# Deeper gather ring, sort turns behind quarters of a tile, and one-hots built from one tensor and two columns of scalars

## The chip, the cores and the metric

The kernel runs on one core of a Trainium2 chip. The core has a matrix engine (TensorE, PE in the profile), three elementwise engines (VectorE or DVE, ScalarE or ACT, GpSimd or POOL), and a queue engine that issues transfers (SyncE or SP). The metric is the device time of one execution in microseconds; shorter is better.

## The reference, cut to what matters

A graph step and a small network. The graph step is the part that the change touches:

```python
h = _layernorm(x) @ weight.T                 # x: 8192 nodes x 512
msgs = edge_weight[:, None] * h[dst]         # 131072 edges
x = x + segment_sum(msgs, src, num_segments=8192)
x = x + ffn(_layernorm(x))                   # seven layers of 160 on a few columns, one-hot results
```

Each edge takes row `dst` of `h`, scales it, and adds it to row `src` of `x`. The edges arrive sorted by `dst`, and have to be added by `src`.

## The kernel before, in words

**Stage one, the product.** `h` is computed in 64 tiles of 128 rows. `multiply(n)` makes four f32 matmuls of 512 columns for tile n, out of `xT` (8 tiles in flight) and `wT`; ScalarE scales the result (`h_rows_out`) and SyncE stores it to `h_dram`. Beside it ScalarE makes the statistics of x, on which `s_sd` tells.

**The sort.** The edges are cut into 4 parts of 128 partitions x 256 (NC) edges. VectorE sorts each part by `src` with a bitonic network: 113 exchange stages. A stage is a "keys" slot (compare into `swap`, L950; copy of the weights, L956; minimum, L958) and a "weights" slot (maximum, L962; predicated copy of the weights, L964). Between stages along the free axis and stages along partitions all keys and weights are transposed on TensorE, 15 times per part (`turn_edges`, L1328 and L1334). During stage one ScalarE copies the turned keys and weights back to SBUF (`turn_out`, L708 and L710); later VectorE copies the turned keys itself (L987). `flip` changes the sign of some keys ahead of a round. The list SORT_SLOTS holds all this in order; every engine walks the same list. Then come "index" (L991, from which POOL may begin to gather the part), "source", and the sums "maxima", "counts", "rows" that make a staircase: tables of which tile of nodes (`tile_of`) and which chunk of 128 edges a step joins, and when a chunk or a tile ends.

`plan()` lays the sort of part 0 and the head of part 1's sort beside stage one. It adds up fixed prices for VectorE and TensorE and gives BEHIND_TILE: behind which tile each turn stands in TensorE's program. HEAD is the number of slots of part 1 that are done before stage two.

**Stage two, the aggregation.** POOL issues 1024 indirect gathers (L630), one per chunk of 128 sorted edges: 128 rows of h, 2 KB each, into one slot of a ring. In parts 0 and 1 the ring has WIDE = T - KEPT + RING = 42 slots: the room of x tiles 32 to 63 (x of those nodes waits in DRAM) and of `wT`, `xT`. In parts 2 and 3 it has RING = 10 slots. Each part has 319 steps (NS). Step i joins one chunk to one tile of nodes: VectorE builds a 128 x 128 matrix with the edge weights at the right rows (`build`, L1064), TensorE multiplies it with the gathered chunk into the PSUM bank of the tile (`add_step`, L1452), up to SR = 8 builds ahead. ScalarE seeds and reads out the banks. A gather into a used slot waits till the steps of the chunk in it are done (`slot_free`). The sort slots of the next part are laid between the steps (`slots_with_steps`), to be through LAST_STEPS = 40 steps before the part begins. Two waits of POOL matter here:

```python
if c == 0:
    pool.wait_ge(s_sd, LOADS)
    near_rows_stored()
if c + 1 == T - KEPT:
    pool.wait_ge(s_mm, T)        # slots under wT and xT: free when stage one is over
```

**Stage three** is the network: it packs marked nodes, runs seven layers, adds the one-hots, and stores.

Of the kernel before, what the change touches and what calls it, by code (L numbers as in the profile page):

```python
# [7 lines left out]
I32 = mybir.dt.int32  # L8
# [7 lines left out]
def gnn_ffn(nc, x, src, dst, edge_weight, gnn_w, ffn_w, ffn_b, x_blocks, out):  # L16
# [8 lines left out]
    P = 128  # L25
# [13 lines left out]
    RING = 10  # L39
    KEPT = 32  # L40
# [4 lines left out]
    FILLED = 44  # L45
# [7 lines left out]
    LAST_STEPS = 40  # L53
# [11 lines left out]
    FAR_BEHIND = 2  # L65
# [9 lines left out]
    def sort_slots():  # L75

        yield "pack", 0, 0
        for k in range(1, QB + 1):
# [5 lines left out]
            yield "flip", k, 0  # L84
# [12 lines left out]
        yield "source", 0, 0  # L97
        for what in ("maxima", "counts", "rows"):
# [7 lines left out]
    ON_TENSOR = ("turn", "maxima summed", "counts summed", "rows summed")  # L106
    assert sum(what == "turn" for what, _, _ in SORT_SLOTS) == TURNS
    assert sum(what == "weights" for what, _, _ in SORT_SLOTS) % 2 == 1

    def plan():  # L110
# [7 lines left out]
        end = start + T * tile + turn * (TURNS + 3)  # L118
        head, is_open = 0, False
        for g in range(2):  # L120
            for at, (what, _, _) in enumerate(SORT_SLOTS):
# [3 lines left out]
                if what in ON_TENSOR:  # L125
                    while n < T - 1 and tensor + tile / 2 < vector:
                        tensor, n = tensor + tile, n + 1
                    behind.append((n, g, what))
                    vector = tensor = max(vector, tensor)
                    vector, tensor = vector + turn, tensor + turn  # L130
# [3 lines left out]
                vector += vector_times.get(what, 0.0)  # L134
                inverts.append(0)
                while b < LOADS and (vector > start + (b * LT + 1) * tile or what in ON_TENSOR and b <= n // LT):
# [15 lines left out]
    BEHIND_TILE, INVERTS, HEAD = plan()  # L152
    HEAD_TURNS = sum(what == "turn" for what, _, _ in SORT_SLOTS[:HEAD])
# [19 lines left out]
    with ctx:  # L173
# [12 lines left out]
        AT_DATA = AT_IOTA + N // 2  # L186
        AT_SORT = AT_DATA + PARTS * 3 * NC
        AT_TAB = AT_SORT + 4 * NC
# [16 lines left out]
        carve = carver(0, AT_EARLY)  # L205
        wT = carve(KD * D).rearrange("p (k f) -> p k f", k=KD)
        all_xT = carve(XS * D)
        xT = all_xT.rearrange("p (s k n) -> p s k n", s=XS, k=KD)
        w_load = all_xT[:, (XS - KD) * D:XS * D].rearrange("p (k f) -> p k f", k=KD)
        carve = carver(AT_EARLY, AT_IOTA)  # L210
# [28 lines left out]
        parts = [(carve(NC, I32), carve(NC), carve(NC)) for _ in range(PARTS)]  # L239
# [1358 lines left out]
```

## Time and profile before

| | us |
|---|---|
| median of 3 runs | 1632.9 (1631.47 to 1633.22) |
| the profiled execution, its own time | 1631.87 |
| its span, first to last instruction | 1630.0 |
| stage one: first to last matmul of L1318 | 15.3 to 244.6 |
| gathers: first and last issue | 192.6 and 1522.3 |
| stage three | about 1529 to 1630 |

The span is 1.9 us below the execution's own time, and that is 1.0 us below the median. The profile's busy share is an average over three stages with different limits: what counts is which wait ends last in each.

### The profile page before, as it was taken

To read this page: it belongs to the slowest core of one execution; us is meant where nothing else is said; L and a number is where in the kernel's file an instruction comes from. 1 tells how busy PE (TensorE), PEld (TensorE's weight loads), DVE (VectorE), ACT (ScalarE), POOL (GpSimd) and SP (SyncE) were. 2 spreads that over 40 slices of the span, in tenths; PEclk is the share of its full clock that TensorE was granted. 3 is DMA by queue.
4 is the path that set the end of the run, shared out by engine and by line. 5 is a ranking of instruction groups with operands and counts; after the bars stand their busy time and mean duration, and the time that the engine had idled before them with its cause. 6 is when DMAs were issued, how large, how long until landed. Compare 5 with 4: busy or idle time off the path is not lost.

```text
span 1630.0 us, 27821 instructions
## 1 busy us (share of the span) xinstructions
PE 1522.7 (93%) x3697; PEld 619.9 (38%) x3698; DVE 1116.9 (69%) x4106; ACT 556.9 (34%) x1223; POOL 1070.4 (66%) x1099
## 2 busy tenths in 40 slices
PE   7999998999989899999998999998999999999995
PEld 3444443444333234343333433333433333333442
DVE  8776648788877878888778777787433333336885
ACT  7887212222222222222222222222234444444332
POOL 2000257777777777777777777777777777777970
PEclk9999999999999999999999999999999999999998
DMA  9886687777999877789988777888877777777563
GB/s 334 300 280 227 213 271 216 205 202 220 307 309 302 285 202 207 199 251 324 309 297 257 207 215 202 246 258 253 252 206 212 209 210 210 208 210 203 181 208 110
DMA packets 162798, 387.79 MB, mean 238 GB/s; under 512 B 32642, under 2 KB 51362, under 8 KB 162466
## 3 DMA queue, kind: packets, MB, share of 16 engines
q0 software_dynamic: 81920, 268.50, 55.4%
q1 hardware_dynamic: 57666, 75.51, 13.8%
q10 hardware_dynamic: 23040, 41.95, 7.7%
q8 instruction: 51, 0.84, 0.2%
q14 instruction: 121, 0.99, 0.2%
HBM read 335.54 MB, written 55.57 MB: 240 GB/s over the span
## 4 chain that ended last, share of the span: by engine, by line
PE 80%; DVE 10%; issue 5%; DMA 2%; DVEq 2%; ACT 0%; POOL 0%; SPq 0%; POOLq 0%; ACTq 0%
PE psum L1452 60%; PE psum L1318 14%; PE psum L1484 3%; DVE rows L1064 3%; DMA rows<-h_rows,rows 2%; DVE rows L964 2%; DVEq L1064 1%; DVE rows L950 1%; DVE rows L956 1%; DVE rows L1144 1%; PE psum L1328 1%; PE psum L1334 1%; DVE rows L962 1%; DVE rows L958 1%; DVE rows L1209 0%
## 5 line engine op out<-in xcount | busy, mean ns | idle before, releaser
L630 POOL DMA_INDIRECT rows<-h_rows,rows x1024 | 1007.7, 984 | 506.2 <-issue 399.3
L1452 PE MATMUL psum<-rows 128*128 x2552 | 1186.2, 608 | 77.5 <-DVE rows L1064 35.3
L1452 PEld LDWEIGHTS psum<-rows 128*128 128x128 f32 x2552 | 443.8, 189 | 775.3 <-issue 767.4
L1064 DVE SCALAR_TENSOR_TENSOR rows<-rows 128x128 f32 (+1 forms) x1276 | 444.9, 351 | 384.4 <-PE psum L1452 271.8
L792 ACT ACTIVATE rows<-psum 128x512 f32<-128x512 f32 x128 | 76.4, 597 | 479.3 <-PE psum L1452 479.3
L1318 PE MATMUL psum<-rows 128*128 128x512 f32 x512 | 223.2, 593 | 0.8 <-ACT rows L689 0.8
L964 DVE COPY_PREDICATED rows<-rows 128x256 f32<-128x256 int32 x407 | 179.7, 442 | 0.0
L774 ACT ACTIVATE psum<-rows 128x512 f32<-128x512 f32 x256 | 153.7, 601 | 8.0
L950 DVE TENSOR_TENSOR rows<-rows 128x128 int32<-128x128 f32 x452 | 129.5, 287 | 19.8 <-ACT rows L708 18.2
L1318 PEld LDWEIGHTS psum<-rows 128*128 128x128 f32 x512 | 96.0, 190 | 114.7 <-issue 114.7
L962 DVE TENSOR_TENSOR rows<-rows 128x128 f32<-128x128 f32 x452 | 128.8, 285 | 0.2
L958 DVE TENSOR_TENSOR rows<-rows 128x128 f32<-128x128 f32 x452 | 128.3, 284 | 0.1
L956 DVE COPY rows<-rows 128x256 f32<-128x256 f32 x407 | 120.5, 296 | 0.6 <-DVE rows L950 0.6
L790 ACT ACTIVATE rows<-psum 128x512 f32<-128x512 f32 x64 | 38.2, 597 | 241.3 <-PE psum L1452 241.3
L828 ACT ACTIVATE rows<-psum 128x512 f32<-128x512 f32 x64 | 38.2, 597 | 181.0 <-PE psum L1452 181.0
L698 ACT ACTIVATE rows<-psum,x_rstd 128x512 f32<-128x512 f32 x64 | 43.9, 686 | 84.2 <-PE psum L1318 83.4
L1484 PE MATMUL psum<-rows 96*96 96x432 f32 x160 | 64.1, 548 | 0.1
L639 POOL TENSOR_SCALAR rows<-rows 128x512 f32<-128x512 f32 x64 | 54.1, 856 | 0.0
L853 ACT ACTIVATE rows<-psum,bias 96x432 f32<-96x432 f32 x48 | 29.6, 616 | 47.7 <-PE psum L1484 44.4
L652 ACT ACTIVATE rows<-rows,x_neg 128x512 bf16<-128x512 f32 x64 | 45.6, 716 | 0.5
L839 ACT ACTIVATE psum<-rows,neg_mean 128x512 f32<-128x512 f32 x64 | 44.2, 691 | 2.1
L652 ACT ACTIVATE rows<-rows 128x512 bf16<-128x512 f32 x68 | 41.8, 620 | 4.5 <-DMA rows<-in_L_gnn_weight 4.5
(152 smaller groups left out, 493.1 us busy)
## 6 DMA issues: line engine op xcount, KB each, us to landing
rows<-in_x_blocks SPq DMA_DIRECT2D x32, 512.0 KB, 4.4
rows<-in_x SPq DMA_DIRECT2D x16, 1024.0 KB, 7.2
h_rows<-rows SPq DMA_DIRECT2D x64, 256.0 KB, 2.9
rows<-h_rows,rows POOLq DMA_INDIRECT x1024, 3.9
summed_rows<-rows ACTq DMA_DIRECT2D x64, 256.0 KB, 5.4
rows<-summed_rows ACTq DMA_DIRECT2D x64, 256.0 KB, 4.4
out<-rows SPq DMA_DIRECT2D x4, 2816.0 KB, 10.7
rows<-in_x ACTq DMA_DIRECT2D x32, 256.0 KB, 5.3
```

Source lines behind the costliest of these rows:

```text
L630: pool.indirect_dma_start(into[:, (c + 1) % n_slots, :], None, h_dram, bass.IndirectOffsetOnAxis(ap=dst_i[g][:, i:i + 1], axis=0),).then_i ...
L652: act.activation(junk[:, sums[0] % 2, :], a, func, bias=bias, accum_out=into).then_inc(s_sum, 1)
L774: act.activation(bank((u + 1) % AGG), given, ACT.Copy).then_inc(s_seed, 1)
L950: dve.tensor_tensor(swap, low, high, ALU.is_gt).then_inc(s_sort[g], 1)
L956: dve.tensor_copy(weights[1 - now], weights_now).then_inc(s_sort[g], 1)
L958: dve.tensor_tensor(to_low, low, high, ALU.min).then_inc(s_sort[g], 1)
L962: dve.tensor_tensor(to_high, low, high, ALU.max).then_inc(s_sort[g], 1)
L964: dve.copy_predicated(both(weights[1 - now], j), swap.unsqueeze(2).to_broadcast(both(weights_now, j).shape), both(weights_now, j)[:, :, :: ...
L1064: dve.scalar_tensor_tensor(spread[:, slot % SR, :], iota_n[:, bass.ds((tile - (g * T + 1)) * P, P)], src_f[g][:, bass.ds(chunk - (g * NC + ...
L1318: last = pe.matmul(bank(n % 4), xT[:, n % XS, k, :], wT[:, k, :], start=(k == 0), stop=(k == KD - 1))
L1452: pe.matmul(banks[:, bass.ds(pe.snap(tile_wanted) % AGG, 1), :].rearrange("p t f -> p (t f)"), spread[:, slot % SR, :], landed_in[:, bass. ...
L1484: return pe.matmul(halves(l)[e], fwT[:, d, l - 1, half_rows[e]], act_f[:, (l - 1) % 2, d, :], start=(d == 0), stop=(d == 1))
```

## The change

- **Ring.** KEPT 32 to 20 and RING 10 to 14: WIDE goes from 42 to 58 slots. 44 tiles of x instead of 32 wait in DRAM; ScalarE's queue loads and stores them. `xT` moves into the last 8 slots of the ring and `wT` out of it, so POOL waits for the end of stage one at chunk 49 instead of chunk 31. The wait on all statistics at chunk 0 becomes one for each x tile whose room a chunk takes. FILLED 44 to 36 (14 fills of rows of `h_dram` instead of 10, two at a time).
- **Turns.** `plan()` has new prices and places turns behind a quarter of a tile (BEHIND_BLOCK) instead of a whole one. VectorE takes the turned weights and the lower half of the turned keys straight from PSUM and copies only the upper half; ScalarE's two copies are gone. The flips ahead of the rounds along partitions become one multiplication by a column of signs in the last stage ahead of the turn (`flip_rows`).
- **Records in the order of steps.** New slot "steps": matmuls with one-hots (`step_hots`) put, for each part, node row and weight of every step in columns (`step_rows`, `step_weights`). "source" is gone.
- **Build.** It reads no table and no register: one tensor and two columns of scalars in the place of two tensors and one column.
- **Far row.** The greatest `dst` of part 0 is found by POOL (`tensor_reduce` over all axes) instead of VectorE and TensorE. POOL's first iota has 1023 columns instead of 8192.
- LAST_STEPS 40 to 64.

```diff
-    RING = 10
-    KEPT = 32
+    RING = 14
+    KEPT = 20
...
-    FILLED = 44
+    FILLED = 36
...
-    LAST_STEPS = 40
+    LAST_STEPS = 64
...
+    def flips_behind(k, j):
+
+        return k >= 7 and k < QB and j == 0
...
-        vector_times = {"pack": 6.0, "flip": 0.3, "keys": 0.65, "weights": 0.65, "turned": 1.9, "maxima": 2.5,
-                        "counts": 2.0, "rows": 2.0, "index": 0.4, "source": 0.8}
-        turn, tile, start = 0.9, 3.43, 15.5
+        vector_times = {"pack": 6.7, "flip": 0.38, "keys": 0.6, "weights": 0.556, "turned": 0.0, "maxima": 3.6,
+                        "counts": 2.0, "rows": 3.2, "steps": 1.0, "index": 0.4}
+        turn, of_block, back, start = 0.75, 0.8575, 0.8, 15.5
...
+            pool.wait_ge(s_edge[0][1], 16)
+            pool.tensor_copy(far_f, dst_i[0]).then_inc(s_far_f, 1)
+            pool.wait_ge(s_far_f, 1)
+            pool.tensor_reduce(far_one[:, :], far_f, mybir.AxisListType.XYZWC, ALU.max).then_inc(s_far, 1)
...
                 if c == 0:
-                    pool.wait_ge(s_sd, LOADS)
                     near_rows_stored()
-                if c + 1 == T - KEPT:
+                if KEPT + c + 1 < T:
+                    pool.wait_ge(s_sd, (KEPT + c + 1) // LT + 1)
+                if c + 1 == WIDE - XS:
                     pool.wait_ge(s_mm, T)
...
-                        if turns <= BY_SCALAR[g]:
-                            dve.wait_ge(s_key_in[g], turns)
-                        else:
-                            weights_now = turned_weights
-                            dve.wait_ge(s_turn_k[g], turns)
-                            dve.tensor_copy(keys_now, turned_keys).then_inc(s_key_in[g], 1)
-                            dve.wait_ge(s_key_in[g], turns)
+                        weights_now, is_turned = turned_weights, True
+                        dve.wait_ge(s_turn_k[g], turns)
+                        first = 6 if j else k - 1
+                        dve.tensor_copy(pairs(keys_now, first)[1], pairs(turned_keys, first)[1]).then_inc(s_key_in[g], 1)
+                        dve.wait_ge(s_key_in[g], turns)
...
-                if i % MORE == 0:
-                    dve.reg_load(walk, tile_of[row_of(g), i:i + MORE])
-                of_tile, of_chunk = ranges(g, i)
-                dve.reg_alu(minus_tile, walk[i % MORE], -1, ALU.mult)
-                dve.reg_alu(of_step, minus_tile, g * T + 1 + g * NC + 1 + i, ALU.add)
-                tile = dve.snap(walk[i % MORE], **of_tile)
-                chunk = dve.snap(of_step, **of_chunk)
                 slot = g * NS + i
                 if slot >= SR:
                     dve.wait_ge(s_done, slot + 1 - SR)
-                dve.scalar_tensor_tensor(spread[:, slot % SR, :], iota_n[:, bass.ds((tile - (g * T + 1)) * P, P)],
-                                         src_f[g][:, bass.ds(chunk - (g * NC + 1), 1)],
-                                         weight[g][:, bass.ds(chunk - (g * NC + 1), 1)].to_broadcast([P, P]),
-                                         ALU.is_equal, ALU.mult).then_inc(s_op, 1)
+                dve.tensor_scalar(spread[:, slot % SR, :], row_q[:, :], step_rows[g][:, i:i + 1],
+                                  step_weights[g][:, i:i + 1], ALU.is_equal, ALU.mult).then_inc(s_op, 1)
...
+            def sum_steps(g):
+
+                pe.wait_ge(s_fin[g], 3)
+                rows_sum, share_sum = bank(ROW_BANK)[:, 0:NSP], bank(SHARE_BANK)[:, 0:NSP]
+                pe.matmul(rows_sum, turned_src[:, 0:P], step_hots[:, 0, :], start=True, stop=False)
+                pe.matmul(rows_sum, turned_src[:, P:NC], step_hots[:, 1, :], start=False, stop=False)
+                pe.matmul(rows_sum, ones[0:T, :], over, start=False, stop=True)
+                pe.matmul(share_sum, turned_wgt[:, 0:P], step_hots[:, 0, :], start=True, stop=False)
+                pe.matmul(share_sum, turned_wgt[:, P:NC], step_hots[:, 1, :], start=False, stop=True).then_inc(s_stair[g], 1)
```

## Rows read from the trace of the kernel before

**Rows 1.** The page: busy time by engine, and the chain that ended last by engine.
```profile
PE 1522.7 (93%) x3697; PEld 619.9 (38%) x3698; DVE 1116.9 (69%) x4106; ACT 556.9 (34%) x1223; POOL 1070.4 (66%) x1099
...
PE 80%; DVE 10%; issue 5%; DMA 2%; DVEq 2%; ACT 0%; POOL 0%; SPq 0%; POOLq 0%; ACTq 0%
```

**Rows 2.** Timeline of POOL: start, length, what, idle time before it (us).
```profile
192.62 1.17 POOL L630 DMA_INDIRECT rows<-h_rows,rows  x1 [183.26 <-issue]
...
232.89 0.95 POOL L630 DMA_INDIRECT rows<-h_rows,rows  x1 [0.30 <-issue]
245.35 0.94 POOL L630 DMA_INDIRECT rows<-h_rows,rows  x1 [11.52 <-PE psum L1318]
...
1522.32 0.95 POOL L630 DMA_INDIRECT rows<-h_rows,rows  x1 [0.30 <-issue]
```

**Rows 3.** Gathers by stretch: its length, busy time (count), granted clock, DMA share.
```profile
245.20:560.00 314.80, 241.00 (x242) 0.99 0.82 256
560.00:870.00 310.00, 236.78 (x241) 1.00 0.83 258
...
1180.00:1440.00 260.00, 197.25 (x207) 1.00 0.73 209
```

**Rows 4.** Weight copies L956, one for each exchange stage, by stretch.
```profile
245.20:560.00 314.80, 37.68 (x120) 0.99 0.82 256
560.00:870.00 310.00, 34.40 (x112) 1.00 0.83 258
```

**Rows 5.** Steps built (L1064) in part 0 and in part 1.
```profile
246.00:561.00 315.00, 110.39 (x318) 0.99 0.83 257
561.00:873.00 312.00, 110.72 (x319) 1.00 0.83 258
```

**Rows 6.** Waits of VectorE up to 192 us: in all, times, longest.
```profile
DVE rows L942 <- ACT rows L708: 18.3, 7, 3.9
DVE rows L950 <- ACT rows L708: 18.2, 7, 4.2
```

**Rows 7.** Timeline of VectorE: two stages in a row, and part 0's "index".
```profile
98.56 0.29 DVE L950 TENSOR_TENSOR rows<-rows 128x128 int32<-128x128 f32 x1
...
99.71 0.29 DVE L950 TENSOR_TENSOR rows<-rows 128x128 int32<-128x128 f32 x1
...
190.48 0.29 DVE L991 TENSOR_SCALAR rows<-rows 128x256 int32<-128x256 int32 x1
```

**Rows 8.** Timeline of TensorE in stage one: 40 matmuls, a turn, the end.
```profile
15.32 34.57 PE L1318 MATMUL psum<-rows 128*128 128x512 f32 x80 [0.78 <-ACT rows L689]
49.73 0.38 PE L1328 MATMUL psum<-ident,rows 128*128 128x128 f32 x2
...
50.16 0.27 PE L1376 MATMUL psum<-ident,far_col 128*1 128x128 f32 x1
...
235.42 9.18 PE L1318 MATMUL psum<-rows 128*128 128x512 f32 x21
```

**Rows 9.** Timeline of the start: POOL's long iota, and VectorE's first pack operation.
```profile
1.19 6.95 POOL L576 IOTA rows<- 128x8192 int16 x1
...
6.93 1.51 DVE L912 TENSOR_SCALAR rows<-rows 128x256 int32<-128x256 int32 x1 [5.00 <-DMA rows<-in_src]
```

**Rows 10.** Timeline: a gather beside a build, a weight copy, and a flip.
```profile
1270.12 0.35 DVE L1064 SCALAR_TENSOR_TENSOR rows<-rows 128x128 f32 x1 [1.06 <-PE psum L1452]
1270.26 1.04 POOL L630 DMA_INDIRECT rows<-h_rows,rows  x1 [0.30 <-issue]
...
990.27 1.08 POOL L630 DMA_INDIRECT rows<-h_rows,rows  x1 [0.30 <-issue]
...
990.91 0.28 DVE L956 COPY rows<-rows 128x256 f32<-128x256 f32 x1
...
1015.29 0.95 POOL L630 DMA_INDIRECT rows<-h_rows,rows  x1 [0.30 <-PE psum L1452]
1015.33 0.22 DVE L942 TENSOR_SCALAR rows<-rows 128x128 f32<-128x128 f32 x1
```

More of the change, by code:

```diff
@@ L96, in sort_slots @@
         yield "index", 0, 0
-        yield "source", 0, 0
-        for what in ("maxima", "counts", "rows"):
+        for what in ("maxima", "counts", "rows", "steps"):
             yield what + " summed", 0, 0
@@ L134, in plan @@
                 vector += vector_times.get(what, 0.0)
+                if what == "weights" and flips_behind(k, j):
+                    vector += 0.25
                 inverts.append(0)
-                while b < LOADS and (vector > start + (b * LT + 1) * tile or what in ON_TENSOR and b <= n // LT):
+                while b < LOADS and (vector > start + (b * LT + 1.7) * tile or what in ON_TENSOR and b <= n // (KD * LT)):
                     inverts[-1], b = inverts[-1] + 1, b + 1
@@ L150, in gnn_ffn @@
     assert FIRST_HOTS + QT // 2 < FIRST_PACK
-    BEHIND_TILE, INVERTS, HEAD = plan()
-    HEAD_TURNS = sum(what == "turn" for what, _, _ in SORT_SLOTS[:HEAD])
+    BEHIND_BLOCK, INVERTS, HEAD = plan()
     def slots_with_steps():
@@ L246, in gnn_ffn @@
         below = other_weights[:, 0:NC // P * T]
-        over = rest[0:T, 0:NSP]
+        over = rest[0:T, 2 * NC - NSP:2 * NC]
+        turned_src, turned_wgt = carve(NC), carve(NC)
+        step_hots = region[:, AT_SORT:AT_SORT + 2 * NSP].rearrange("p (b i) -> p b i", b=2)
+        assert 2 * NSP <= 4 * NC - NSP and NC == 2 * P
         carve = carver(AT_TAB, REGION)
@@ L444, in progress @@
             steps = turns = buffer = 0
-            for what, _, _ in SORT_SLOTS:
+            for what, k, j in SORT_SLOTS:
                 if what == "turn":
@@ L449, in progress @@
                     turns += 1
-                steps += SORT_STEPS.get(what, 0)
+                steps += steps_of(what, k, j)
                 buffer ^= what == "weights"
@@ L492, in _ @@
                         load_pair(n // 2 + XS // 2)
-                    late = next(to_fill, None) if n >= 2 * (LOADS - FIRST_LOADS) else None
-                    if late is not None:
+                    for late in islice(to_fill, 2 if n >= 2 * (LOADS - FIRST_LOADS) else 0):
                         sp.dma_start(h_dram[late * P:(late + 2) * P, :], x[late * P:(late + 2) * P, :]).then_inc(s_fill, 16)
@@ L992, in sort_edges @@
                                           ).then_inc(s_index, 1)
-                    elif what == "source":
-                        src_i = keys[1 - now].bitcast(I32)
-                        step(dve.tensor_scalar(src_i, keys[now].bitcast(I32), KEY, N - 1,
-                                               ALU.logical_shift_right, ALU.bitwise_and))
-                        dve.tensor_copy(src_f[g], src_i).then_inc(s_fin[g], 1)
                     elif what == "maxima":
@@ L1318, in multiply @@
                     last = pe.matmul(bank(n % 4), xT[:, n % XS, k, :], wT[:, k, :], start=(k == 0), stop=(k == KD - 1))
-                last.then_inc(s_mm, 1)
+                    if k == KD - 1:
+                        last.then_inc(s_mm, 1)
+                    for block, g, what in BEHIND_BLOCK:
+                        if block == KD * n + k:
+                            of_sort(g, what)
             def turn_edges(g, turn):
@@ L1382, in of_sort @@
                     sum_rows(g)
+                elif what == "steps summed":
+                    sum_steps(g)
             turn_w()
@@ L1386, in _ @@
                 multiply(n)
-                for tile, g, what in BEHIND_TILE:
-                    if tile == n:
-                        of_sort(g, what)
             def turn_layer(l):
```

182 lines of the change are left out of this document (102 added, 80 removed).

## The prediction

> **What bounds the kernel now.** The page comes first, and it misleads: TensorE is busy 93% of the span and holds 80% of the chain that ended last, POOL is busy 66% and holds none of it [rows 1]. The timeline of POOL shows the bound. The first gather is issued at 192.6 us, one wait of 11.5 us ends when stage one does, and from 245.35 us to 1522.32 us there follow 992 more, each with the same 0.30 us of idle time ahead of it and nothing longer [rows 2]. That is 1277.0 / 992 = 1.287 us a gather. POOL waits for no slot and for no sort: in stage two it is never stopped, and nothing that doesn't touch its pace or its start can move 1522.3 us, behind which the last steps and stage three take a fixed 107.7 us (to 1630.0). TensorE runs in its shadow: its small waits for chunks, spread over the steps, are what the chain adds up as TensorE.
>
> Gathers by stretch show what the pace is made of [rows 3]: without sort beside it one takes 197.25 / 207 = 0.953 us, with sort 0.996 and 0.983. The excess over 0.953 is 10.4 + 7.2 = 17.6 us in two stretches with 232 stages [rows 4]: a stage of five VectorE operations costs POOL 0.076 us, or 15 ns an operation.
>
> **The ring and its wait.** The sum starts where POOL is stopped. Before, 31 gathers are out when stage one ends; after, POOL may issue 49. Their start is early enough: "index" stands at 190.5 us [rows 7], and it moves forward (below, to about 165), while 49 gathers take 49 x 1.3 = 64 us. So at the end of stage one POOL stands 18 chunks further: 18 x 1.287 = -23.2 us. The start of the gathers by itself is worth nothing: POOL then waits for the end of stage one some 25 us instead of 11.5. The other conditions (36 tiles stored, 14 fills, statistics) are met near tile 38, at about 155 us, and bind less than "index". The 24 more stores and 36 more loads of 256 KB run on ScalarE's queue beside a DMA share of 0.8; the gathers have the same length at 0.82 as elsewhere, so I cost them at nothing; what hides them is a ring 13 deep or more. Without that cover each late chunk would cost its lateness.
>
> **The end of stage one.** It is at 235.42 + 9.18 = 244.6 us [rows 8]. A matmul takes (49.73 - 15.32) / 40 = 0.86 us, a turn 50.16 - 49.73 = 0.43 us. The new plan puts four more turns (part 1's) ahead of the end: 1.7 us. sum_steps is five matmuls of 320 columns, 5 x 0.54 = 2.7 us, and two more transposes 0.1 us. Unhindered, stage one ends at 249.1 us: the lower bound.
>
> But every turn stands at a fixed place in TensorE's program and waits for VectorE's sort. Before, VectorE was always early and waited: 18.3 + 18.2 = 36.5 us over 14 turns, 2.6 us each [rows 6]. After, the turns are set by VectorE's expected pace, and TensorE waits where it is late; behind TensorE's wait the rest of stage one is queued, and behind that POOL. VectorE's path to "index": 190.5 less the waits (36.5), less the start that POOL's iota held up (1.2, below), less the far operations (seven short ones, about 1.6), plus 15 turns at 0.8 us (0.4 for the transposes of the keys, 0.3 for half a copy, 0.1 for semaphores), plus 3 for full-width flips and PSUM operands: 166 us. Walking plan() with its own prices gives 159.1 us there, and the last turn of part 1's head behind block 226 at 228.8 us. VectorE is thus some 5 us late (7 less 2 of slack where the plan lets it wait), and the end is 228.8 + 5 + 0.4 + 29 x 0.86 = 259 us; if the plan is right, 254. Between 249.1 and 260 I take 257, near the VectorE end, because it sets the pace in most turns: +12.4 us.
>
> **The stages moved.** HEAD goes from 28 slots to 130: 45 stages of part 1 instead of 12 are done in stage one. 33 x 0.076 = -2.5 us of POOL's excess. VectorE has little work late in stage one today, which is the cover for this.
>
> **The build.** Its time on VectorE is not on POOL's path; what it does to gathers is. A build today starts at 1270.12 and runs over the start of a gather at 1270.26, which takes 1.04 instead of 0.945 us: it ends 0.83 us behind the build. In the stretch without sort builds are nearly alone: (0.953 - 0.945) x 207 = 1.7 us for 258 steps, 7 ns a build. The new form reads one tensor. The nearest rows are the copy L956 and the flip L942, also of one tensor, which run at two elements a cycle by their lengths (256 in 0.28, 128 in 0.22 us). Behind the copy at 990.91 the gather of 990.27 takes 1.08 us, and ends again a fixed time (0.15) behind it; beside the flip at 1015.33 the gather stays at 0.95 [rows 10]. So the new build may also hold a gather at a later point, and is shorter (0.28 to 0.35). Bounds for the difference: -7 ns (it never holds one) and +15 ns (as an operation of the sort), -9 to +19 us over 1276. I take +4 ns, the flip being nearer in form than the copy: +5 us.
> The Trainium skill (SBUF - State Buffer, section "SBUF: two separate sides") says that a VectorE operation in a two-port mode and a GpSimd operation exclude each other for the whole instruction. The rows show less: most overlapped gathers keep 0.945 us. By the rule each build met by a gather would stop it, and the sum would end well on the slower side.
>
> **On VectorE itself** the build loses 0.0 to 0.07 us and its register work; "maxima", "rows" and "steps" gain some 3 us a part and "source" loses 0.6. LAST_STEPS moves part 1's end of sort from step 279 to 255. None of it is on POOL's path while sorts are done in time.
>
> **Sum.** -23.2 + 12.4 - 2.5 + 5 = -8.3 us. The profiled execution: 1631.87 - 8.3 = 1623.6; the median stands 1.0 higher: 1624.6 us.
>
> **Rivals.**
> *The steps can't follow (no gain or slower).* In part 2 the ring shrinks to 14 slots, and gather 517 needs the slot of chunk 507, whose last step is about number 632. POOL is there at 257.7 + 468 x 1.287 = 860 us. Steps begin at 259.3, so they must take 0.950 us or less. Today they take 627 / 637 = 0.984 us [rows 5], although the ring is full enough: TensorE waits for builds queued behind sort slots. It has 0.86 us plus 24 turns and the sums, 0.895. VectorE loses 33 stages (38 us at 1.15 us [rows 7]), some of each build, and the register work. I expect 0.935. At an unchanged pace the stop is 259.3 + 632 x 0.984 - 860 = 21 us, and the time 1646. It decides from 0.950 us on. Chance 0.19, spread over 1625 to 1646.
> *POOL's reduction holds VectorE (slower).* The iota on POOL runs to 8.14 us, and VectorE's operation of 6.93, which takes 0.29 elsewhere [rows 7], ends 0.30 us behind it [rows 9]. The new tensor_reduce starts at about 9 us, when the sort does. Nothing in the rows prices it: at least the 0.4 us of an operation of 256 columns; if it walks partition by partition at iota's 6.95 / 8192 us an element, 32768 elements take 28 us. Turns wait for VectorE, so each microsecond goes to the end of stage one and to POOL: 1624.6 + 28 = 1652. It decides from 8 us on. Against it: the new plan prices the pack at 6.7 us. Chance 0.14.
> The Trainium skill (GPSIMD Engine Reference, "Cross-partition - where GPSIMD wins") measures 247,699 ns for a partition reduction of [128, 2048]; an estimate by columns is 31 us for 256. No run here shows it yet.
> *Builds hold gathers often (slower).* At one in five and 0.15 us, as the long gathers of [rows 10] suggest, 1276 builds cost 38 us instead of 5: 1658. The gain is gone from 10 ns a build on. Chance 0.10.
> *More gain.* TensorE hardly waits (end at 250) and builds cost nothing: -23.2 + 5.4 - 2.5 - 4 = -24: 1609. Chance 0.09.
> *The parts cancel* within 3 us, by a few waits of each kind: 0.08.
>
> **How the numbers follow.** The forecast, with 1618 to 1631 as its own range, has 0.40. The range of 1608 to 1656 leaves out less than 2 in 10: the ends of the last rivals but one. A difference of 0.2%, 3.3 us, is about what a measurement of this kernel can tell from none. Faster: 0.37 of the forecast, 0.09, and 0.02 of the first rival: 0.48. Same: 0.03, 0.08 and 0.05: 0.16. Slower: 0.36.
>
> **What would show it.** POOL's timeline: first gather near 165, one long wait ahead of gather 49, ended by TensorE at about 257; any later wait ahead of gather 517 or so is the first rival. Gathers of 0.95 us in the stretch without sort, where 0.97 and more would be the third. The reduction's length at 9 us and VectorE's copies beside it. TensorE's waits for VectorE in stage one: some 8 us. The last gather at about 1514. The forecast is wrong if POOL has a second stop, or if its 0.30 us between gathers changes.

## The result, and the profile after

The changed kernel takes 1689.4 us (median of 4 runs, 1674.8 to 1696.3) against 1632.2: a ratio of 1.0339, interval 1.0271 to 1.0408. Ratios here compare only the runs of a kernel that lie within 1.5% of its fastest, while medians and ranges are of all its runs. It is 3.4% slower where 0.5% faster was forecast, and outside the range. The profiled execution has a span of 1686.8 us; 1621.7 was forecast (1630.0 - 8.3), 65.1 us less. The experiments ran on four chips, each time beside the kernel before, whose median lies between 1634 and 1650 us there: from one chip to another the ratios compare better than the times.

The page of the changed kernel, as [rows 1]:
```profile
PE 1540.3 (91%) x3744; PEld 639.6 (38%) x3745; DVE 1109.3 (66%) x4158; ACT 548.6 (33%) x1193; POOL 1118.6 (66%) x1102
...
PE 71%; DVE 21%; issue 5%; DMA 2%; POOL 0%; ACT 0%; POOLq 0%; SPq 0%; DVEq 0%
```
POOL is 48 us busier and VectorE has 21% of the chain instead of 10%. POOL's timeline, as [rows 2], says where:
```profile
166.29 1.19 POOL L662 DMA_INDIRECT rows<-h_rows,rows  x1 [157.79 <-DMA h_rows<-rows]
...
256.96 0.96 POOL L662 DMA_INDIRECT rows<-h_rows,rows  x1 [21.42 <-PE psum L1337]
...
1560.34 0.95 POOL L662 DMA_INDIRECT rows<-h_rows,rows  x1 [0.30 <-issue]
```
The first gather (165 forecast), one stop ahead of the fiftieth, its end (257.7 forecast): all as foreseen, and no second stop. But the 974 gathers behind it have a pitch of (1560.34 - 256.96) / 974 = 1.338 us, not 1.287, so that the last comes 46 us behind the forecast 1514. The idle time between them is still 0.30 us; the gathers themselves are longer. By stretch, as [rows 3]:
```profile
258.00:560.00 302.00, 235.56 (x218) 1.00 0.85 270
560.00:870.00 310.00, 241.90 (x223) 0.99 0.82 253
870.00:1140.00 270.00, 209.33 (x199) 0.99 0.78 233
1180.00:1440.00 260.00, 196.63 (x209) 1.00 0.75 218
```
And the weight copies, one for each stage of the sort (L982 now), as [rows 4]:
```profile
258.00:560.00 302.00, 30.74 (x102) 1.00 0.85 270
560.00:870.00 310.00, 29.62 (x98) 0.99 0.82 253
```
Without sort beside it a gather takes 0.941 us, no more than before (cut-off gathers left out, the mean is 0.948 us, and 0.956 in the kernel before): the new build holds hardly any, as 10 gathers of this stretch are longer than 0.96 us, where it was 28 before. With sort it takes 1.081 and 1.085. That excess is 30.4 + 32.1 = 62.5 us over 200 stages, 0.31 us a stage, where [rows 3, 4] had 0.076.

The rest of the 65 us is behind the last gather: 126.4 us to the end instead of 107.7. Timelines of POOL and of VectorE there:
```profile
1561.32 39.73 POOL L671 TENSOR_SCALAR rows<-rows 128x512 f32<-128x512 f32 x48
```
```profile
1566.68 19.64 DVE L1163 TENSOR_SCALAR rows<-rows 128x216 bf16<-128x216 int16 x1 [8.78 <-PE psum L1480]
```
One small VectorE operation (its fifteen fellows take 6.3 us together) needs 19.64 us, while POOL runs its scalings without a break. In the kernel before POOL runs them without a break as well, from the same 0.99 us behind the last gather, and the sixteen operations together take 6.40 us. Timelines of POOL and of VectorE before:
```profile
1523.31 21.86 POOL L639 TENSOR_SCALAR rows<-rows 128x512 f32<-128x512 f32 x24
```
```profile
1529.03 6.40 DVE L1144 TENSOR_SCALAR rows<-rows 128x216 bf16<-128x216 int16 x16 [3.88 <-PE psum L1452]
```

### The profile page after: what moved, and what is told of

It is laid out like the page before. It is cut to its first block, busy times and chain, and to the rows that moved or that the text cites. A ratio compares the mean times of both kernels' runs of the same rounds, so it can differ in the third digit from the quotient of the medians.

```text
span 1686.8 us, 24194 instructions
## 1 busy us (share of the span) xinstructions
PE 1540.3 (91%) x3744; PEld 639.6 (38%) x3745; DVE 1109.3 (66%) x4158; ACT 548.6 (33%) x1193; POOL 1118.6 (66%) x1102
## 4 chain that ended last, share of the span: by engine, by line
PE 71%; DVE 21%; issue 5%; DMA 2%; POOL 0%; ACT 0%; POOLq 0%; SPq 0%; DVEq 0%
PE psum L1480 53%; PE psum L1337 11%; DVE rows L1085 4%; DVE rows L994 3%; PE psum L1512 3%; DVE rows L982 3%; DVE rows L978 2%; DVE rows L984 2%; DVE rows L988 2%; DVE rows L1163 2%; DMA rows<-h_rows,rows 1%; PE psum L1349 1%; DVE rows L1006 1%; PE psum L1353 0%; POOL rows L662 0%
## 5 line engine op out<-in xcount | busy, mean ns | idle before, releaser
L662 POOL DMA_INDIRECT rows<-h_rows,rows x1024 | 1062.2, 1037 | 490.6 <-issue 225.2
L1480 PEld LDWEIGHTS psum<-rows 128*128 128x128 f32 x2552 | 455.1, 190 | 782.0 <-issue 772.5
L1085 DVE TENSOR_SCALAR rows<-row_q,rows 128x128 f32<-128x128 f32 x1276 | 440.8, 356 | 308.3 <-PE psum L1480 287.8
L994 DVE COPY_PREDICATED rows<-rows 128x256 f32<-128x256 int32 x392 | 171.2, 437 | 0.0
L1337 PEld LDWEIGHTS psum<-rows 128*128 128x128 f32 x512 | 95.5, 190 | 112.6 <-issue 112.4
L1006 DVE COPY rows<-psum 128x128 f32<-128x128 f32 x60 | 17.5, 291 | 167.1 <-PE psum L1349 166.9
L982 DVE COPY rows<-rows 128x256 f32<-128x256 f32 x392 | 116.0, 296 | 0.0
L978 DVE TENSOR_TENSOR rows<-rows 128x128 int32<-128x128 f32 x392 | 110.2, 281 | 0.8
L988 DVE TENSOR_TENSOR rows<-rows 128x128 f32<-128x128 f32 x392 | 110.0, 281 | 0.0
L984 DVE TENSOR_TENSOR rows<-rows 128x128 f32<-128x128 f32 x392 | 109.9, 280 | 0.1
L1512 PE MATMUL psum<-rows 96*96 96x432 f32 x160 | 67.9, 575 | 0.1
```

What stands on the lines that cost most here:

```text
L662: pool.indirect_dma_start(into[:, (c + 1) % n_slots, :], None, h_dram, bass.IndirectOffsetOnAxis(ap=dst_i[g][:, i:i + 1], axis=0),).then_i ...
L978: dve.tensor_tensor(swap, low, high, ALU.is_gt).then_inc(s_sort[g], 1)
L982: dve.tensor_copy(weights[1 - now], weights_now).then_inc(s_sort[g], 1)
L984: dve.tensor_tensor(to_low, low, high, ALU.min).then_inc(s_sort[g], 1)
L988: dve.tensor_tensor(to_high, low, high, ALU.max).then_inc(s_sort[g], 1)
L994: dve.copy_predicated(both(weights[1 - now], j), swap.unsqueeze(2).to_broadcast(both(weights_now, j).shape), both(weights_now, j)[:, :, :: ...
```

## A lock between two engines

What makes the gathers long is seen where six long ones follow each other. POOL's timeline of the changed kernel:
```profile
654.14 1.36 POOL L662 DMA_INDIRECT rows<-h_rows,rows  x1 [0.30 <-issue]
655.80 1.35 POOL L662 DMA_INDIRECT rows<-h_rows,rows  x1 [0.30 <-PE psum L1480]
657.45 1.35 POOL L662 DMA_INDIRECT rows<-h_rows,rows  x1 [0.30 <-issue]
```
and VectorE's beside it, one stage of the sort with its two builds:
```profile
654.39 0.28 DVE L984 TENSOR_TENSOR rows<-rows 128x128 f32<-128x128 f32 x1
654.59 0.34 DVE L1085 TENSOR_SCALAR rows<-row_q,rows 128x128 f32<-128x128 f32 x1
654.85 0.28 DVE L988 TENSOR_TENSOR rows<-rows 128x128 f32<-128x128 f32 x1
655.05 0.44 DVE L994 COPY_PREDICATED rows<-rows 128x256 f32<-128x256 int32 x1
655.39 0.34 DVE L1085 TENSOR_SCALAR rows<-row_q,rows 128x128 f32<-128x128 f32 x1
655.64 0.28 DVE L978 TENSOR_TENSOR rows<-rows 128x128 int32<-128x128 f32 x1
655.85 0.28 DVE L982 COPY rows<-rows 128x256 f32<-128x256 f32 x1
656.05 0.28 DVE L984 TENSOR_TENSOR rows<-rows 128x128 f32<-128x128 f32 x1
```
L978 is the comparison, L982 the weight copy, L984 the minimum, L988 the maximum, L994 the predicated copy. Each starts some 80 ns before the one ahead of it has ended: there is no break. The minimum ends at 654.67 and the gather of 654.14 at 655.50, 0.82 us behind it (the rows are rounded); the gather of 655.80 ends at 657.15, 0.82 us behind the next minimum (656.33). So a gather that is held ends 0.82 us behind a minimum, the next starts 0.30 us later, and by then (1.12 us behind the minimum) the next stage has begun (0.97 us behind it). It is held again, and the gathers take the stage's period, 1.66 us, for their own 1.25. I call that the lock. Told by this arithmetic alone (held again if the next stage begins within 1.12 us) it is theory 4 of the expectations, formed after e8; e10 will refute the arithmetic, not the lock.

It can be counted. For all gathers issued from 262 to 1150 us: held is one longer than 0.953 us that ends 0.78 to 0.835 us behind a minimum. "Next stage" is the median time from a minimum's end to the next comparison's start. The mean is of all gathers behind the end of stage one, with sort beside them or not; the time is the median of all runs.

| run | next stage, us | held | of them followed by a held one | mean gather, ns | median time, us |
|---|---|---|---|---|---|
| before | 1.175 | 67 | 3 | 983 | 1632 |
| after | 0.975 | 140 | 98 | 1033 | 1689 |
| e1 | 0.971 | 150 | 108 | 1041 | 1697 |
| e2 | 0.986 | 131 | 93 | 1047 | 1708 |
| e3 | 0.984 | 130 | 93 | 1048 | 1703 |
| e4 (before, fixed) | 0.984 | 134 | 93 | 1050 | 1717 |
| e5 | 1.166 | 143 | 65 | 1026 | 1664 |
| e6 | 1.092 | 155 | 102 | 1034 | 1702 |
| e7 (before, fixed) | 1.104 | 141 | 84 | 1035 | 1703 |
| e8 | 0.972 | 154 | 111 | 1038 | 1675 |
| e9 | 1.239 | 31 | 0 | 974 | 1638 |
| e10 | 1.114 | 11 | 0 | 974 | 1634 |
| e11 | 1.239 | 28 | 0 | 975 | 1613 |
| e12 | 0.976 | 128 | 86 | 1029 | 1712 |
| e13 | 1.114 | 10 | 0 | 974 | 1615 |
| e14 (before, fixed) | 1.130 | 24 | 0 | 977 | 1647 |
| e15 | 1.239 | 36 | 0 | 974 | 1639 |
| e16 | 1.091 | 68 | 0 | 976 | 1640 |

The kernel before beside these took 1650 (e1 to e4), 1636 (e5 to e8), 1634 (e9 to e12) and 1642 us (e13 to e16; one of its 27 runs there took 8840.7 us). In the changed kernel held gathers make up 56 of the 83 us by which the gathers of the table exceed 0.945 us each; in the kernel before 18 of 31.

## The experiments

The theories at first: (1) the register work of the old builds left gaps on VectorE, in which gathers got through; (2) the form of the build; (3) something else in the change.

**e1.** Register work put back, unused:
```
...
+if i % MORE == 0:
+    dve.reg_load(walk, tile_of[row_of(g), i:i + MORE])
+dve.reg_alu(minus_tile, walk[i % MORE], -1, ALU.mult)
+dve.reg_alu(of_step, minus_tile, g * T + 1 + g * NC + 1 + i, ALU.add)
```


> The changed kernel with one thing put back: VectorE's queue again loads the tile numbers (one register load in every group) and works out two register values ahead of every build, as before; nothing reads them, and the build itself stays the new one-tensor form at fixed columns. Theory 1, gaps: before, this register work left about 0.10 us of VectorE's time empty between the last sort operation of a slot and the build, and in such a gap a gather that stands ready gets its start; the changed kernel has no gap there, the sort operations run back to back and hold gathers until their chain ends. Then the gap comes back here, the gathers' mean falls from 1.037 us towards 0.985, the last gather comes near 1515 to 1525 instead of 1560, and the time is near 1640 to 1650 (about 45 us less than the changed kernel). Theory 2, the form of the build: the old build read two tensors and was itself the place where gathers started or were let go in step; then nothing comes back here, mean 1.03 to 1.04 and 1680 to 1695. Theory 3, the rest of the change (the ring, the turned copies, the sort's new order) causes it: also 1680 to 1695.


Ratio 1.0267 (1.0204 to 1.0330), mean 1041 ns: nothing came back.

**e2.** The old form, fixed columns:
```
-dve.tensor_scalar(spread[:, slot % SR, :], row_q[:, :], step_rows[g][:, i:i + 1],
-                  step_weights[g][:, i:i + 1], ALU.is_equal, ALU.mult).then_inc(s_op, 1)
+dve.scalar_tensor_tensor(spread[:, slot % SR, :], row_q[:, :], step_rows[g][:, i:i + 1],
+                         step_weights[g][:, i:i + 1].to_broadcast([P, P]), ALU.is_equal, ALU.mult).then_inc(s_op, 1)
```


> The changed kernel with the build back as an operation on two tensors (the row numbers, and the weight's column broadcast along the row), at fixed columns and without register work. Theory 1 (gaps from register work): no gap comes back, gathers' mean stays 1.03 to 1.04 and the time 1680 to 1695, or some 5 us more if the build itself holds gathers. Theory 2 (the form of the build): the gathers' mean falls to about 0.985 and the time to 1640 to 1650. Theory 3 (the rest of the change): 1680 to 1695.


1708 us beside 1650, mean 1047 ns. Even its fastest run, 1680.2 us, lies above the slowest of the kernel before, 1654.0: theory 2 falls.

**e3.** Both.


> The changed kernel with both put back: register work ahead of every build and the build on two tensors. All else (ring of 14, order of steps, turns, far rows) is the change's. Theories 1 and 2 both give a gathers' mean near 0.985, the last gather near 1515 to 1525 and 1635 to 1650. Theory 3 (the rest of the change makes gathers longer): mean 1.03 or more, 1680 to 1700.


Ratio 1.0290 (1.0217 to 1.0363): neither. But the build still starts 202 ns behind the minimum's start, where it was 390 in the kernel before: the register work, whose results nobody read, ran hidden and made no gap. e1 and e3 hadn't tried theory 1.

**e4.** The kernel before, builds at fixed addresses, no register work; it leaves out the choice of the right columns:
```
...
-iota_n[:, bass.ds((tile - (g * T + 1)) * P, P)], src_f[g][:, bass.ds(chunk - (g * NC + 1), 1)], ...
+iota_n[:, 0:P], src_f[g][:, i % NC:i % NC + 1], weight[g][:, i % NC:i % NC + 1].to_broadcast([P, P])
```


> The kernel before with its build at fixed addresses and without the register work ahead of it; the form on two tensors stays. It leaves out the choice of the right columns, so its output isn't the reference's; the amount of work in the engines is the same but for the register work. Theory 1 (the register work made the gaps in which gathers start): the gathers' mean rises from 0.984 to 1.02 to 1.04 us, and the kernel gets slower by 30 to 50 us, 1660 to 1685. Theories 2 and 3: no slower, 1625 to 1635.


Ratio 1.0369 (1.0289 to 1.0450), which is 61 us of 1650 (67 between the medians), with every other part of the old kernel in place. The distance from minimum to build fell from 390 to 202 ns, and 93 of 134 held gathers are followed by a held one. So the loss needs no other part of the change: it comes when the addresses out of registers go, with their register work, which e1 and e3 found to do nothing by itself. Not all of it is the gathers': their pitch is 1.354 us instead of 1.287, and from the last gather to the end it is 132.7 us instead of 107.7, with one VectorE operation of 16.77 us in it.

**e5.** The changed kernel, builds addressed through registers (always to the same columns), with the register work that this needs:
```
...
+none = dve.snap(minus_tile, min_val=0, max_val=1)
+at = dve.snap(of_step, min_val=i, max_val=min(i + 1, NSP - 1))
-row_q[:, :], step_rows[g][:, i:i + 1], step_weights[g][:, i:i + 1]
+row_q[:, bass.ds(none, P)], step_rows[g][:, bass.ds(at, 1)], step_weights[g][:, bass.ds(at, 1)]
```


> In e1 and e3 the register work put back was hidden: the build still started 202 ns after the minimum of a sort stage, without a gap, so they didn't try theory 1. In the kernel before the gap of 105 ns stood ahead of builds whose columns come out of registers, and e4, without them, lost the gap and 67 us. Here the changed kernel gets register work and builds whose three operands are addressed through registers (they always come to the same columns as the fixed ones); the form stays the new one on one tensor. Theory 1 (a gap in VectorE's chain lets POOL's waiting gather start): the start of the build lies about 390 ns behind that of the minimum (L984 here), the gathers' mean falls from 1.037 to about 0.985, and the time comes near 1640 to 1655. Theory 3 (something else of the change makes gathers longer): the gap is there, the mean stays at 1.03 or more, the time 1685 to 1705.


The gap is back (391 ns from minimum to build); the time is 1663.7, ratio 1.0161 (1.0134 to 1.0189): about half of the loss. But hardly by the gathers. The last one comes at 1554.4 us, 6 us before that of the changed kernel, and their pitch is 1.331 us instead of 1.338; 19 us are won behind it, where it is 107.4 us to the end instead of 126.4 and no operation is long.

**e6.** The changed kernel with a wait behind the minimum:
```
 dve.tensor_tensor(to_low, low, high, ALU.min).then_inc(s_sort[g], 1)
 done += 3
+dve.wait_ge(s_sort[g], done)
```


> The changed kernel with one wait more in each sort stage: behind the minimum VectorE waits for its own completion before it goes on to the build. It should leave a gap of about 35 ns, as between other operations that wait for the one just ahead, and cost VectorE some 115 ns a stage, with 500 stages 58 us of a queue that idles for longer than that behind the gathers. Theory 1: gathers find the gap, mean about 0.985 to 1.0, 1640 to 1660 (slower by 0 to 10 than that if 35 ns is short for some). Theory 3: mean 1.03 or more, 1690 to 1710.


Ratio 1.0345 (1.0288 to 1.0402). The wait leaves 37 ns, and changes nothing for the gathers: their pitch is 1.338 us as without it. (It also stands in stage one, where it delayed the first gather to 180.7 us and the fiftieth to 272.8.)

**e7.** e4 with that wait.


> The kernel of e4 (the one before with builds at fixed addresses; it leaves out the choice of the right columns) and the same wait behind the minimum of each sort stage. Theory 1: the gap comes back, gathers' mean from 1.049 to about 0.985 to 1.0, and the time from 1717 to 1645 to 1670. If it was something else in the register work than the gap, it stays at 1700 to 1725.


Ratio 1.0393 (1.0352 to 1.0435): no. "Gaps" as such don't explain it; the column "followed by a held one" came out of these runs.

**e8.** The tail:
```
 pool.wait_ge(s_mark, h + 1)
+if h:
+    pool.wait_ge(s_hotf, h + 1)
```


> The changed kernel with POOL held, ahead of its 8 scalings of each later quarter of the tail, until VectorE has made the one-hots of that quarter. In the changed kernel POOL ran 32 of these back to back behind the last gather (24 us), and one VectorE operation beside them took 19.6 us instead of some 0.3. If that is what made the last stage 126.5 us instead of 107.7, the stage behind the last gather falls by 10 to 19 us and the time to 1670 to 1682 (gathers' mean unchanged at 1.03 to 1.04). If the long operation is an effect without cost, the time stays at 1685 to 1697.


1674.7 us (1674.0 to 1675.6), 14.7 less, and four runs within 1.6 us; by the ratios, 1.0236 instead of 1.0339, it is 17 us. 106.5 us from the last gather to the end, 19.9 less. Timelines of POOL and of VectorE in e8:
```profile
1567.02 12.42 POOL L673 TENSOR_SCALAR rows<-rows 128x512 f32<-128x512 f32 x16
1579.87 15.45 POOL L673 TENSOR_SCALAR rows<-rows 128x512 f32<-128x512 f32 x16 [0.43 <-DVE rows L1165]
```
```profile
1572.14 7.55 DVE L1165 TENSOR_SCALAR rows<-rows 128x216 bf16<-128x216 int16 x16 [8.49 <-PE psum L1482]
```
The sixteen operations take 7.55 us instead of 25.98.

**e9.** Waits behind minimum and predicated copy, beside the gathers alone (`spaced` is set behind stage one):
```
 dve.tensor_tensor(to_low, low, high, ALU.min).then_inc(s_sort[g], 1)
 done += 3
+if spaced:
+    dve.wait_ge(s_sort[g], done)
...
 dve.copy_predicated(...).then_inc(s_sort[g], 1)
 done += 2
+if spaced:
+    dve.wait_ge(s_sort[g], done)
```


> Theory 4, a lock, formed from the runs so far: a gather that becomes ready while the sort's two-input operations run back to back ends about 0.82 us behind the end of the minimum; the next gather starts 0.30 us later, 1.12 us behind that end. If the next stage's first operation has begun by then, that gather is held too. Time from the end of a minimum to the start of the next stage, median: 1.175 us in the kernel before (3 of 67 held gathers followed by a held one), 1.166 in e5 (65 of 143), 1.092 in e6 (102 of 155), 0.975 in the changed kernel (98 of 140), 0.984 in e4 (93 of 134). Here the changed kernel waits for its own completion behind the minimum and behind the predicated copy of a stage, in the second sort beside the gathers alone: the time is to be about 1.22 us. Theory 4: hardly any held gather is followed by a held one (under 15 in 100), the gathers' mean falls to 0.98 to 1.00, and the time to 1640 to 1655. Rival, gaps in general (the more empty time on VectorE, the more gathers get through): a second gap takes the mean from e6's 1.034 to 1.02 at best, time 1675 to 1690. Rival, neither: 1690 or more.


As theory 4 had it: no held gather is followed by a held one, the mean is 974 ns, the last gather comes at 1504.4 us. Median 1638.0 us, ratio 0.9926 (0.9883 to 0.9969). More waiting on VectorE made the kernel some 50 us faster.

**e10.** The second of the two waits alone.


> The same wait behind the predicated copy alone (second sort, beside the gathers): the time from the end of a minimum to the next stage is to be about 1.10 us, short of what a gather needs. Theory 4: still locked, more than half of the held gathers followed by a held one, mean 1.03 to 1.04, 1685 to 1700. Gaps in general: as for e9 with one gap, about 1680.


The expectation was wrong: median 1633.7, ratio 0.9969 (0.9935 to 1.0003), mean 974, no lock, with the next stage 1.114 us away. So the 1.12 us don't decide, and theory 4 in its simple form falls.

**e11.** e9 and e8.


> e9 and e8 together: the waits of e9, and POOL held in the tail until the one-hots of its quarter are made. If the two losses are separate and theory 4 is right, 1625 to 1640, level with the kernel before or up to 0.7% faster. If theory 4 is wrong, 1670 to 1680 as in e8.


1613.1 us (1612.4 to 1614.8), ratio 0.9875 (0.9858 to 0.9891): faster than both kernels.

**e12.** The changed kernel, `RING = 10`, `KEPT = 32`.


> The changed kernel with the ring's sizes as before (10 slots instead of 14, 32 tiles kept instead of 20); the new build and order of steps stay. By the prediction's own step the ring gives 18 chunks of start, worth 1.29 us each: without it the time is 20 to 25 us longer than the changed kernel's, about 1710. If the earlier start had no worth because the end of stage one or the lock sets the time anyway, 1685 to 1697. If the ring itself brings on the lock, 1640 to 1665.


1711.6, ratio 1.0408 (1.0339 to 1.0477): the ring doesn't bring on the lock.

**e13.** e10 and e8.


> e10 and e8 together: one wait a stage, behind the predicated copy, and the tail's wait. e10 escaped the lock although theory 4's simple form (1.12 us from the minimum to the next stage) had it locked; its times then scattered from 1614 to 1640, as e9's did, where e11 with the tail's wait lay within 2.4 us. If that scatter is the tail's, this kernel comes at 1610 to 1616 with as little scatter. If e10 was a lucky state of the lock, some of its runs lie over 1650.


1615.4 us (1611.6 to 1616.4), ratio 0.9830 (0.9812 to 0.9849), on a chip where the kernel before took 1642. The times of e9, e10 and e16 scatter over 26 to 35 us, from 1610, 1614 and 1616 up; with the tail's wait, e11 and e13 lie within 5 (e15, below, within 7). In the profiles of e9 and e10 the long operation of the tail is there again (19.7 and 18.8 us; last gather to end 127.0 and 124.4), in that of e16, a low run, it is not (113.9). So the scatter is very likely that of the tail, also in the changed kernel; only one run of each kernel has a profile.

**e14.** e4 with e10's wait.


> The kernel of e4 (the one before with builds at fixed addresses; it leaves out the choice of the right columns), which was 67 us slower than the one before, with e10's wait behind the predicated copy. Theory 4, refined (the lock needs the run of overlapped operations from the predicated copy through the build into the next stage; a wait behind the copy cuts it): no more lock, gathers' mean from 1.049 to 0.97 to 0.985, 1625 to 1645. If e10's escape hangs on something else of the changed kernel: 1695 to 1720.


1647.3 beside 1642.1, ratio 0.9992 (0.9960 to 1.0024), where e4 had 1.0369; mean 977, no held gather followed by a held one. The lock and its cure are the same in the old kernel.

**e15.** e11, ring as before.


> The kernel of e11 with the ring's sizes as before (10 slots, 32 tiles kept). In the locked kernel the ring was worth 22 us (e12, 1711.6 against 1689.4). The prediction's step has it worth 18 chunks by 1.29 us, 23 us: 1633 to 1640 here. If without the lock the steps of the tail or another wait set the end, less than 10 us: 1613 to 1623.


1638.5, ratio 0.9976 (0.9962 to 0.9990): 23.1 us more than e13 on the same chip. (e13 has one wait less a stage, at the same mean gather.) Against e11, its twin but for the ring, the ratios differ by 1.0%, 16 us. POOL's timeline of e15 at the end of stage one, and its last gather:
```profile
256.54 0.96 POOL L662 DMA_INDIRECT rows<-h_rows,rows  x1 [40.27 <-PE psum L1346]
...
1522.28 0.95 POOL L662 DMA_INDIRECT rows<-h_rows,rows  x1 [0.30 <-issue]
```
The gather of 256.54 is the thirty-fourth, as in e12: with the small ring the changed kernel's condition stops POOL at chunk 33, where the kernel before was stopped at chunk 31. So e12 and e15 take back 16 chunks of the start, not 18.

**e16.** The wait behind the maximum:
```
 dve.tensor_tensor(to_high, low, high, ALU.max).then_inc(s_sort[g], 1)
+if spaced:
+    dve.wait_ge(s_sort[g], done + 1)
```


> The changed kernel with the stage's wait at a third place, behind the maximum (ahead of the predicated copy), in the second sort beside the gathers. The time from a minimum to the next stage is to be about 1.09 us, as in e6 and e10. Refined theory (the run from the predicated copy on into the next stage is what counts): still locked as e6, mean 1.03 or more, 1685 to 1700. If any gap but one right behind the minimum frees gathers: mean 0.98, 1625 to 1645.


The refined theory fell, its rival held: no lock, mean 976, ratio 0.9939 (0.9901 to 0.9977). e6 and e16 have the same next stage (1.09 us), the same 35 ns of gap and VectorE's work; only its place differs. First e6, POOL and VectorE:
```profile
460.13 1.48 POOL L662 DMA_INDIRECT rows<-h_rows,rows  x1 [0.30 <-issue]
```
```profile
460.10 0.29 DVE L978 TENSOR_TENSOR rows<-rows 128x128 int32<-128x128 f32 x1
460.30 0.29 DVE L982 COPY rows<-rows 128x256 f32<-128x256 f32 x1
460.50 0.29 DVE L984 TENSOR_TENSOR rows<-rows 128x128 f32<-128x128 f32 x1
```
then e16:
```profile
408.12 1.07 POOL L662 DMA_INDIRECT rows<-h_rows,rows  x1 [0.30 <-issue]
```
```profile
408.08 0.28 DVE L978 TENSOR_TENSOR rows<-rows 128x128 int32<-128x128 f32 x1
408.29 0.28 DVE L982 COPY rows<-rows 128x256 f32<-128x256 f32 x1
408.49 0.28 DVE L984 TENSOR_TENSOR rows<-rows 128x128 f32<-128x128 f32 x1
408.69 0.55 DVE L1090 TENSOR_SCALAR rows<-row_q,rows 128x128 f32<-128x128 f32 x1
```
The gather starts 0.03 to 0.04 us into the comparison in both, and in both the gather ahead of it was a held one. In e6 it ends 0.82 us behind the minimum's end; in e16 only 0.42 behind it, and now the build at 408.69 takes 0.55 us instead of 0.34. The same meeting goes POOL's way in e16 and VectorE's in e6. One rule fits the runs, with a proviso for breaks at the minimum itself: a gather is held once more if VectorE has run without a break since the minimum that let the last one go. A break right at that minimum doesn't count at 37 ns (e6, e7), counts in part at 107 (e5, next stage 1.166) and fully at 105 in the kernel before (next stage 1.175). Why so little lies between the last two stays open. It isn't the moment of the start: of the gathers that follow a held one and start about 0.05 us ahead of the next comparison, 64 of 66 are held in e5 and 2 of 41 in the kernel before. The two have different forms of the build, and no run tried both forms at this gap. What in the chip makes the rule isn't shown.

## Why the prediction was wrong

**The step that failed** is the price of a sort stage: "a stage of five VectorE operations costs POOL 0.076 us, or 15 ns an operation". It was read from [rows 3, 4] and carried over as a constant, though it was the price in one timing of VectorE against POOL. "Its time on VectorE is not on POOL's path; what it does to gathers is" looked at the build alone. The build itself costs gathers hardly anything, less than the +5 us of the sum; but without the gap ahead of it the stages repeat every 1.66 us, and the price of a stage is 0.31 us. Shown by e4 (take the gap out of the old kernel: the pitch goes from 1.287 to 1.354 us) and by e9, e10, e14 and e16 (break the run elsewhere). From e8 to e11 it is 1674.7 to 1613.1; by ratios to the kernel before on each chip 1.0236 to 0.9875, 3.6%, 59 us. The pitches say the same: (1.338 - 1.279) x 974 = 57 us. Putting the gap back as it was didn't cure the new kernel's gathers (e5), so the gap is not the whole story of why the kernel before escaped.

**The fixed 107.7 us** was the second wrong step: 126.4, because one VectorE operation waited 19.64 us beside POOL's scalings. That POOL runs them back to back isn't enough, since the kernel before does so too. Of the profiled runs without the tail's wait, the long operation is missing in three: the kernel before, e5 (both with builds addressed through registers) and e16. It is there in all others (16.7 to 19.9 us), e4, e7 and e14 of the old kernel among them. What decides it stays open. e8 takes it away, for 19.9 us in the profile and 14.7 in the medians.

**The sum without the two.** e13 is the changed kernel with both losses taken out. Its POOL timeline, and gathers by stretch:
```profile
258.98 0.97 POOL L662 DMA_INDIRECT rows<-h_rows,rows  x1 [18.75 <-PE psum L1344]
...
1505.01 0.94 POOL L662 DMA_INDIRECT rows<-h_rows,rows  x1 [0.30 <-issue]
```
```profile
258.00:560.00 302.00, 230.29 (x233) 1.00 0.87 282
560.00:870.00 310.00, 236.52 (x242) 1.00 0.86 279
```
Its last gather is at 1505.0, 9 us ahead of the forecast 1514: the pitch is 1.279 us instead of 1.287, which over 974 gathers is 8 us. The mechanism of the sum stands. How good its number was is less sure: e13's profile is 7 us below the forecast 1621.7, but by the ratios to the kernel before e11 and e13 gain 20 and 28 us, not 8.3.

**The ring.** -23.2 us forecast for 18 chunks. That POOL stands 18 gathers further when stage one ends is counted (stopped ahead of gather 50 instead of 32), with no stop behind. The worth of one chunk was tested with 16: from e11 to e15 the last gather moves by 19.0 us, and with the end of stage one at the same time (256.54 instead of 257.22 us) it would be 19.7, 1.23 us a chunk where 1.287 was forecast. The step is right. The medians of e15 and e13 differ by 23.1 us, more than 16 chunks explain (20.6 at the forecast's price); that this meets the forecast for 18 is chance.

**The end of stage one.** 257 forecast, 256.2 measured, but not made as I wrote. TensorE's waits for VectorE and its timeline in the changed kernel:
```profile
PE psum L1349 <- DVE rows L988: 1.3, 4, 0.4
...
PE psum L1349 <- DVE rows L917: 0.5, 1, 0.5
```
```profile
45.20 0.44 PE L1349 MATMUL psum<-ident,rows 128*128 128x128 f32 x2
45.56 0.44 PE L1353 MATMUL psum<-ident,rows 128*128 128x128 f32 x2
45.84 1.02 PE L1337 MATMUL psum<-rows 128*128 128x512 f32 x2
...
243.60 12.61 PE L1337 MATMUL psum<-rows 128*128 128x512 f32 x29
```
Late turns cost about 2 us, not 8. Most turns take 0.64 us (45.20 to 45.84) where they took 0.43 [rows 8], 3 us over 19 turns. An error of one sign met smaller ones of the other, so a part of this hit is luck.

**The rivals.** The steps followed: one stop, no second. The reduction didn't hold VectorE, in POOL's timeline:
```profile
7.46 0.80 POOL L610 CROSS_LANE_REDUCE far_one<-rows 128x1 f32<-128x256 f32 x1
```
0.80 us, against my 28 at worst. The Trainium skill (GPSIMD Engine Reference, "Cross-partition - where GPSIMD wins") led to an estimate of 31 us; the row decides against it for this instruction. "Builds hold gathers often" had the victim right and the size near (38 us; the last gather came 46 us late), and the cause wrong: the gathers without sort beside them show that builds hardly hold any.
The Trainium skill (SBUF - State Buffer, section "SBUF: two separate sides") says that a VectorE operation in a two-port mode, or with two inputs out of SBUF against a GpSimd operation that reads SBUF, shares ports with GpSimd, and that whichever starts first has them for its whole instruction. The rows agree that one side blocks and that it can be either (the build of 0.55 us in e16). They show more than the section tells: a gather is held past the ends of the comparison and of the copy to that of the minimum. I take it that each next operation had begun by then, which no run tried. I had set this page aside because most gathers weren't stopped in the kernel before; it spoke against the change, and for a reason that I had not asked about.

## What to carry to other kernels

Where two engines exclude each other, the cost of an overlap isn't a price an operation: compare the period of the one with the period of the other, and ask where the released one comes back. The periods alone don't decide it (e6 and e16 have the same, and only one locks), so try a break at several places. A faster instruction or a gap removed can close the window; a wait of some 0.1 us on the engine with time to spare can open it (here one line, worth about 60 us). And a stage behind the bound that one profile shows is "fixed" only until two engines in it meet differently: here it was 107 to 135 us from the last gather to the end.

## What the runs showed of the hardware

- A comparison, a copy and a minimum on VectorE, each starting some 80 ns before the last has ended, held a gather of 0.945 us until 0.82 us behind the end of the minimum, mostly 1.35 us in all, up to 1.79, though the build and the maximum followed without a break.
- It can be VectorE that waits: a build of 0.34 us took 0.55 where the gather went first (e16).
- Operands addressed through registers open a gap of 105 ns behind the operation ahead; the same register work without such operands opens none (e1, e3). Waiting for the own last operation opens 35 to 37 ns.
- A run of POOL's scalings (32 of 128x512 in 24 us, 0.75 us each) kept a VectorE operation of 128x216 waiting 16.7 to 19.9 us in most profiled runs, and not in three others.
